# Layer 3 of a four-layer chain: split float32r product replaced by a plain float32 product on four 32-row groups of TensorE

## What is computed

```python
x = x + L0(x)   # x W^T + (x A0[label]) B0^T * 0.5      A0 rank 32, float32
x = x + L1(x)   # eight thresholds: quantise x with the step and zero point of its level
x = x + L2(x)   # x weight[adapter]^T, 1024x1024, float32
x = x + L3(x):
    B_sel = B[adapter_ids]                        # 16 x 1024
    A_sel = A[adapter_ids]                        # 1024 x 16
    Bx = einsum('bni,bri->bnr', x, B_sel)         # rank 16
    out = einsum('bnr,bor->bno', Bx, A_sel)
```

## Time and profile before

| | us |
|---|---|
| median of 3 runs (467.7 to 470.2) | 469.33 |
| the profiled execution's own time | 469.18 |
| its span, first to last instruction | 467.4 |
| PE busy | 456.0 (98%) |
| DVE busy | 414.8 (89%) |
| ACT busy | 326.7 (70%) |

### The profile page before, as it was taken

The page is one execution under the profiler, slowest core; times in us unless marked ns, Lnnn a source line. Parts: engine busy times, 40 slices in busy tenths (PEclk is TensorE's granted clock), DMA queues, the critical chain, the costliest instruction groups (busy, mean ns, idle before and its releaser), DMA issues.

```text
span 467.4 us, 7302 instructions
## 1 busy us (share of the span) xinstructions
PE 456.0 (98%) x3006; PEld 414.1 (89%) x3006; DVE 414.8 (89%) x394; ACT 326.7 (70%) x273; POOL 7.9 (2%) x17
## 2 busy tenths in 40 slices
PE   6999999999899999999999999999999999999996
PEld 5999999889898899989998899988998899988884
DVE  4789899999899997889799996899959999999983
ACT  5596999986498748957299653997249866665730
POOL 1000000000000000000000000010000000000000
PEclk9899999999999999999999999999999999999999
DMA  7983340476229534456326562193322432244242
GB/s 290 307 350 101 69 126 1 109 202 241 69 91 236 192 126 157 88 182 210 140 90 141 191 221 91 68 260 109 142 99 90 156 115 79 86 175 168 103 157 90
DMA packets 17940, 69.15 MB, mean 148 GB/s; under 512 B 2420, under 2 KB 3444, under 8 KB 13044
## 3 DMA queue, kind: packets, MB, share of 16 engines
q1 hardware_dynamic: 17044, 62.41, 37.5%
q0 software_dynamic: 864, 6.29, 7.0%
HBM read 54.01 MB, written 8.39 MB: 134 GB/s over the span
## 4 chain that ended last, share of the span: by engine, by line
PE 85%; DVE 6%; ACT 3%; issue 3%; DMA 1%; SPq 1%; DVEq 0%; ACTq 0%
PE l_ps L830 39%; PE l_ps L765 32%; PE l_ps L845 6%; DVE quant L627 2%; PE bx_ps L864 2%; DVE cand L601 2%; PE bx_ps L791 1%; DMA w_sb<-w 1%; PE l_ps L775 1%; PE l_ps L881 1%; ACT cand L438 1%; DVE quant L621 1%; ACT mask L448 1%; PE bx_ps L798 1%; PE bx_ps L871 1%
## 5 line engine op out<-in xcount | busy, mean ns | idle before, releaser
L830 PE MATMUL l_ps<-x,w_sb 128*128 128x256 f32 x896 | 197.0, 380 | 1.0 <-DVE x L678 0.6
L830 PEld LDWEIGHTS l_ps<-x,w_sb 128*128 128x128 f32 x896 | 169.2, 190 | 26.1 <-issue 3.6
L627 DVE COPY_PREDICATED quant<-mask,cand 128x2048 f32<-128x2048 int8 (+2 forms) x77 | 144.4, 1876 | 1.9 <-ACT mask L448 1.6
L438 ACT ACTIVATE cand<-x,inv_delta 128x2048 f32<-128x2048 f32 (+2 forms) x88 | 134.6, 1529 | 8.8 <-DVE quant L621 7.0
L448 ACT ACTIVATE mask<-magnitude,thr_bias 128x2048 fp8e5<-128x2048 f32 (+2 forms) x77 | 117.8, 1530 | 20.2 <-DVE quant L627 19.5
L601 DVE TENSOR_SCALAR cand<-cand,delta 128x2048 f32<-128x2048 f32 (+2 forms) x88 | 87.4, 993 | 11.8 <-ACT cand L438 11.4
L609 DVE TENSOR_SCALAR cand<-cand,lower,upper 128x2048 f32<-128x2048 f32 (+2 forms) x88 | 92.6, 1053 | 0.4
L765 PE MATMUL l_ps<-x_hi,w_hi 128*128 128x256 f32 x512 | 87.0, 292 | 4.2 <-DVE x_lo L564 1.8
L765 PE MATMUL l_ps<-x_hi,w_lo 128*128 128x256 f32 x512 | 83.0, 284 | 0.0
L765 PE MATMUL l_ps<-x_lo,w_hi 128*128 128x256 f32 x512 | 82.9, 284 | 0.0
L765 PEld LDWEIGHTS l_ps<-x_hi,w_hi 128*128 128x128 f32 x512 | 72.1, 193 | 9.3 <-issue 3.3
(11 more groups left out here) (64 smaller groups left out, 244.1 us busy)
## 6 DMA issues: line engine op xcount, KB each, us to landing
w_sb<-w SPq DMA_DIRECT2D x31, 1024.0 KB, 4.9
out<-x SPq DMA_DIRECT2D x32, 256.0 KB, 2.2
x_raw<-x SPq DMA_DIRECT2D x15, 512.0 KB, 6.3
x_lo<-x_raw POOLq DMA_DIRECT2D x6, 1024.0 KB, 8.2
a_raw<-a SPq DMA_DIRECT2D x8, 512.0 KB, 3.5
w_sb<-w SPq DMA_DIRECT2D x7, 512.0 KB, 7.4
b_sb<-b SPq DMA_DIRECT2D x8, 256.0 KB, 2.6
a_raw<-a SPq DMA_DIRECT2D x8, 128.0 KB, 6.2
```

What stands on the lines that cost most here:

```text
L438: act.activation(cand[:, c % CANDS, 0:n], x2_unit(u), ACT.Identity, bias=ROUND, scale=inv_delta[:, k:k + 1]).then_inc(rounded, 1)
L627: dve.copy_predicated(y, mask[:, m % MASKS, 0:n].bitcast(I8), t).then_inc(merged, 1)
L830: last = nc.tensor.matmul(l2_bank(b, q)[:, i * S:(i + 1) * S], w2_tile(b, o)[:, k * P:(k + 1) * P], x2[:, b % SLOTS, k * S:(k + 1) * S], s ...
```

## The change

Layer 3 becomes a plain float32 product. `a3_raw` now holds the second matrix (16 rows, padded with 16 zero rows) four times, on partitions 0-31, 32-63, 64-95 and 96-127. `bx_sum` is filled so that `sum_bx` puts Bx on all four groups of 32 as well; ACT copies it once to `bx_sb`. Quarter q of the output is then computed from partitions 32q to 32q+31 alone, so that the four quarters use four different row groups of the array; the matmuls take turns over the quarters. The splitting of `a3` and of `bx` on ACT and DVE is gone. Batch 7 takes the same way as the others: four column groups in `low_rank3`, then `drain_bx`, `sum_bx` and `copy_bx`. `b3_sb` is half as wide. `load_adapter(b)` waits for the end of layer 3 of the batch before, since layer 3 now reads `a3_raw` itself.

```diff
@@ load_adapter on SP
                 else:
                     sp.wait_ge(bx_done, b)
-                    sp.wait_ge(a3_split_done, b)
+                    sp.wait_ge(l3_done, 4 * b)
@@ ACT
-            def split_a3(b):
-                act.wait_ge(a3_loaded, (b + 1) * 16)
-                if b > 0:
-                    act.wait_ge(l3_done, 4 * b)
-                act.activation(a3_split[:, :], a3_raw[:, :], ACT.Copy).then_inc(a3_hi_done, 1)
...
-            def split_bx(b):
-                if b < B - 1:
-                    act.wait_ge(bx_sum_done, b + 1)
-                else:
-                    act.wait_ge(bx_done, b + 1)
+            def copy_bx(b):
+                act.wait_ge(bx_sum_done, b + 1)
                 if b > 0:
                     act.wait_ge(l3_done, 4 * b)
-                act.activation(bx_split[:, :], bx_whole(b), ACT.Copy).then_inc(bx_hi_done, 1)
+                act.activation(bx_sb[:, :], bx_ps[:, S:2 * S], ACT.Copy).then_inc(bx_copied, 1)
...
-            split_a3(B - 1)
-            split_bx(B - 1)
+            drain_bx(B - 1)
+            copy_bx(B - 1)
@@ DVE
-            def split_a3(b):
-                dve.wait_ge(a3_hi_done, b + 1)
-                dve.scalar_tensor_tensor(a3_split[:, :], a3_split[:, :].bitcast(F32), not_a3_hi[:, 0:1], a3_raw[:, :],
-                                         ALU.mult, ALU.add).then_inc(a3_split_done, 1)
-
-            def split_bx(b):
-                dve.wait_ge(bx_hi_done, b + 1)
-                dve.scalar_tensor_tensor(bx_split[:, :], bx_split[:, :].bitcast(F32), not_bx_hi[:, 0:1], bx_whole(b),
-                                         ALU.mult, ALU.add).then_inc(bx_split_done, 1)
@@ PE
-                n = 4 if b < B - 1 else 2
-                w = P // n
                 for k in (2 * q, 2 * q + 1):
-                    rows = slice(k % n * w, (k % n + 1) * w)
-                    last = nc.tensor.matmul(bx_ps[rows, 0:S], b3_sb[:, k, 0:w], x3[:, k * S:(k + 1) * S],
-                                            start=(k < n), stop=(k >= T - n))
+                    rows = slice(k % 4 * QUAD, (k % 4 + 1) * QUAD)
+                    last = nc.tensor.matmul(bx_ps[rows, 0:S], b3_sb[:, k, :], x3[:, k * S:(k + 1) * S],
+                                            start=(k < 4), stop=(k >= 4))
...
-            def layer3(b, q):
-                if q == 0:
-                    pe.wait_ge(bx_split_done, b + 1)
-                    pe.wait_ge(a3_split_done, b + 1)
-                on_x3 = b == B - 1 and q == 3
+            def layer3(b, order=range(4)):
+
+                pe.wait_ge(bx_copied, b + 1)
+                pe.wait_ge(a3_loaded, (b + 1) * 16)
                 for i in range(2):
-                    o = 2 * q + i
-                    last = nc.tensor.matmul(l3_bank(b, q)[:, i * S:(i + 1) * S], a3_split[:, o * P:(o + 1) * P],
-                                            bx_split[:, :], start=not on_x3, stop=not on_x3 or i == 1)
-                last.then_inc(l3_done, 1)
+                    for q in order:
+                        o = 2 * q + i
+                        rows = slice(q * QUAD, (q + 1) * QUAD)
+                        on_x3 = b == B - 1 and q == 3
+                        last = nc.tensor.matmul(l3_bank(b, q)[:, i * S:(i + 1) * S], a3_raw[rows, o * P:(o + 1) * P],
+                                                bx_sb[rows, :], start=not on_x3, stop=not on_x3 or i == 1)
+                        if i == 1:
+                            last.then_inc(l3_done, 1)
...
-            for q in LAST_ORDER:
-                layer3(B - 1, q)
+            sum_bx(B - 1)
+            layer3(B - 1, LAST_ORDER)
```

More of the change, by code:

```diff
@@ L78, in build @@
         low_parts = sb("low_parts", [P, S], F32)
-        b3_sb = sb("b3_sb", [P, T, 2 * QUAD], F32)
+        b3_sb = sb("b3_sb", [P, T, QUAD], F32)
         bx_parts = sb("bx_parts", [P, S], F32)
         a3_raw = sb("a3_raw", [P, D], F32)
-        a3_split = sb("a3_split", [P, D], F32R)
-        bx_split = sb("bx_split", [P, S], F32R)
+        bx_sb = sb("bx_sb", [P, S], F32)
         ident = sb("ident", [P, P], F32)
@@ L125, in build @@
         param_step = sem("param_step")
-        marks_ready = sem("marks_ready")
         diag_added = sem("diag_added")
@@ L151, in build @@
         x3_done = sem("x3_done")
-        a3_hi_done = sem("a3_hi_done")
-        a3_split_done = sem("a3_split_done")
         bx_done = sem("bx_done")
@@ L156, in build @@
         bx_sum_done = sem("bx_sum_done")
-        bx_hi_done = sem("bx_hi_done")
-        bx_split_done = sem("bx_split_done")
+        bx_copied = sem("bx_copied")
         l3_done = sem("l3_done")
@@ L327, in _ @@
             pool.memset(low_sum[:, :], 0.0).then_inc(sums_zeroed, 1)
-            pool.memset(bx_sum[:, :], 0.0).then_inc(sums_zeroed, 1)
-            pool.wait_ge(sums_zeroed, 2)
+            pool.wait_ge(sums_zeroed, 1)
             pool.wait_ge(fold_ready, 1)
@@ L333, in _ @@
             pool.tensor_copy(low_sum[:, 3 * QUAD:4 * QUAD], fold[:, :]).then_inc(sums_ready, 1)
-            pool.tensor_copy(bx_sum[:, 0:3 * R3].rearrange("p (q r) -> p q r", q=3),
-                             fold[:, 0:R3].unsqueeze(1).to_broadcast([P, 3, R3])).then_inc(sums_ready, 1)
+            pool.tensor_copy(bx_sum[:, :].rearrange("p (q r) -> p q r", q=4),
+                             fold[:, :].unsqueeze(1).to_broadcast([P, 4, QUAD])).then_inc(sums_ready, 1)
             def add_x(b):
@@ L473, in between @@
                         split_batch(s + 2)
[L474 to L477, removed]
+                    if j == 3 and s + 2 < B:
+                        drain_low(s + 2)
                     if j == 4 and s + 2 < B:
@@ L482, in between @@
                         drain_l0(s + 1, 0)
-                        split_bx(s - 1)
+                        copy_bx(s - 1)
                         if s + 1 < B - 1:
@@ L486, in between @@
                 elif u == LAST:
-                    if j == 2:
-                        split_a3(s - 1)
                     if j == 3:
@@ L644, in between @@
                         drain_l2(s - 1, 1)
-                    if j == 3:
-                        split_a3(s - 1)
                     if j == 4:
@@ L683, in _ @@
             dve.wait_ge(ident_ready, 1)
-            for mark, low in ((not_bx_hi, slice(QUAD, 2 * QUAD)), (not_a3_hi, slice(R3, 2 * R3))):
-                dve.tensor_reduce(mark[:, :], ident[:, :].rearrange("p (g c) -> p g c", g=2)[:, :, low],
-                                  mybir.AxisListType.XY, ALU.add, negate=True).then_inc(marks_ready, 1)
             dve.tensor_reduce(fold[:, :], ident[:, :].rearrange("p (g r) -> p r g", g=4),
@@ L725, in _ @@
             dve.wait_ge(param_step, 6)
-            dve.wait_ge(marks_ready, 2)
             for u in range(len(UNITS)):
@@ L731, in _ @@
                 finish(b - 1, q)
-            split_a3(b)
             for q in range(4):
                 drain_l2(b, q)
-            split_bx(b)
             for q in LAST_ORDER:
@@ L905, in _ @@
                     if i == 4:
-                        for q in range(4):
-                            layer3(s - 1, q)
+                        layer3(s - 1)
             for q in range(4):
@@ L915, in _ @@
             last_layer2(1, (1, 2, 3))
-            for q in range(4):
-                layer3(B - 2, q)
+            layer3(B - 2)
             last_layer2(2)
@@ L943 @@
     b3 = np.asarray(L3_cond_B).reshape(-1, R3, T, P).transpose(0, 3, 2, 1)
-    b3 = np.concatenate([b3] * 3 + [np.zeros_like(b3)], axis=3)
+    b3 = np.concatenate([b3, np.zeros_like(b3)], axis=3)
     a3 = np.asarray(L3_cond_A).transpose(0, 2, 1)
-    a3 = np.concatenate(([a3] * 3 + [np.zeros_like(a3)]) * 2, axis=1)
+    a3 = np.concatenate([a3, np.zeros_like(a3)] * 4, axis=1)
     arrays = {
@@ L957 @@
         "w2": tiles_of_weights(L2_cond_weight).reshape(-1, 4, 2, P, T * P).transpose(0, 1, 3, 2, 4),
-        "b3": b3.reshape(-1, P, T * 2 * QUAD),
+        "b3": b3.reshape(-1, P, T * QUAD),
         "a3": a3,
```

11 lines of the change are left out of this document (removed).

## The result

| | before | after |
|---|---|---|
| median, us (5 runs each) | 469.27 (467.7 to 470.2) | 472.22 (471.56 to 473.26) |
| profiled execution's own time | 469.18 | 472.22 |
| its span | 467.4 | 470.4 |

The ratio is 1.0079, with a 95% interval from 1.0056 to 1.0102: slower by more than 0.5%, as forecast, and 0.2 us from the forecast time. That nearness is luck. Two errors of opposite sign cancel in it, and the rows tell them apart.

What follows compares the result with a forecast made beforehand. PE's queue was taken to bound the kernel from 81 us on. Layer 3 in batches 0 to 6 (+2.0) and the last batch (+1.2) made +3.2 us on 469.18, so 472.4; range 469.0 to 476.0.

Steps and rivals of the forecast that it cites:

- What bounds the kernel: Whole kernel: from 81 us on PE's queue sets the time; DVE's removed splits, 14.1 us busy, are worth nothing.
- Layer 3, batches 0 to 6: Layer 3 on PE: 16 float32 passes in four row groups cost 1.24 against 0.96 us, +0.28 a batch, +2.0 for seven.
- The row of the identity passes: Four passes after `low_rank3` of batch 7, after a switch with a full load ahead: 1.06 us, taken as layer 3's price.
- the way back: Tile behind layer 3: leaving the split array costs another 0.18 us, as after `low_rank3` (3.06 instead of 2.88).
- `low_rank3` of batch 7, held by DVE's add: End of the kernel: its last quarter waits for DVE's add at 459.45, so it ends at 460.10, 0.43 earlier.
- The last batch: Batch 7: layer 3 starts 0.54 us later and quarters end together, so DVE's first add comes +1.17 us later.
- `load_adapter` at nothing: SP's queue: two load issues, 0.53 us each, ahead of the stores cost nothing; the loads have 2 us or more cover.
- The rival of the late adapter load: Batch 7: late batch 6 stores delay DVE's adds, or `b3` comes late: +1 us on the forecast, 473.4; chance 0.03.
- Serial loads: Layer 3: row groups' weight loads go one at a time, 2.30 us a batch, sum +11.1, 480.3; chance 0.10.
- no overlap: Layer 3: the four row groups do not overlap, 3.46 us a batch, sum +19.9, 489.1; chance 0.05.
- Free switch: Layer 3: row-group loads run ahead under full-width tiles, 0.86 us a batch; with the end +0.4, 469.6; chance 0.12.
- The base: Whole kernel: the forecast was added to the profiled execution's 469.18 us, leaving out the 0.15 higher median of 469.33.

Runs made afterwards that it cites:

- before_no_dve_split: Kernel before without DVE's halves of the two splits, low parts left out of layer 3: 468.53 us, ratio 1.0002 to before.
- layer3_twice: Changed kernel with layer 3's eight matmuls issued twice in batches 0 to 6: 479.05 us, ratio 1.0223 to the kernel before.
- one_row_group: Changed kernel with all eight layer 3 matmuls on partitions 0 to 31 in place of four row groups: 496.84 us, ratio 1.0606 to before.
- two buffers: Changed kernel with two buffers for the second matrix, so the adapter load is issued well ahead of the stores: 472.26 us, ratio 1.0063 to before.
- after_filled_gap: Changed kernel with eight small identity matmuls, results unused, in PE's wait at 9.6 us: 471.97 us, ratio 1.0081 to before.
- quarter_by_quarter: Changed kernel with layer 3's loops swapped, both halves of a quarter before the next quarter: 472.86 us, ratio 1.0073 to before.

## Why the prediction was right, and where it was not

- *What bounds the kernel.* Right. DVE lost 12.8 us of work for nothing, and the chain of waits is as full of PE as before. The 0.4 us wait for DVE in layer 2 stayed where the earlier trace rows put it. `before_no_dve_split` confirms it from the other side, with the same 371.52 us from the first pass of layer 2 to the end of layer 3 of batch 6.
- *Layer 3, batches 0 to 6: +0.28 a batch, +2.0.* Right: +0.31 by the chain, 1.97 and 1.95 over the whole stretch in the two pairs of profiles. The row of the identity passes (1.06) gave 1.08, the way back 0.18 gave 0.19. `layer3_twice` shows the split into 0.86 and 0.41, and `one_row_group` shows that the four groups are what saves 2.56.
- *`low_rank3` of batch 7, held by DVE's add.* Right as a mechanism, and 1.48 for 1.45 where the stores are in time. In the changed kernel itself, it was wrong.
- *The last batch, +1.17.* With two buffers, DVE's first add stands 11.74 us after the end of layer 3 of batch 6, and 10.33 before: +1.41, of which 0.19 is the way back that the forecast has under layer 3. That is +1.2. So the two terms that the forecast added up, 3.2, measure 1.97 + 1.41 = 3.4 where the stores are in time.
- *The step that failed, though the time came out: `load_adapter` at nothing.* The prediction saw that two loads would be issued in front of the stores and priced them by their issues and their own deadlines, with "2 us or more" of cover. It did not price what stands behind them: DVE's adds wait for the stores to land, and a store behind the 512 KB load landed after 5.4 and not 2.2 us. The rival of the late adapter load had the place right, down to the condition that DVE's last add must slip, and its price nearly (+1; it is +1.3 in the profile, 0.7 in the trace of `after_filled_gap`, 0.3 in that of `quarter_by_quarter`), but got 0.03 of the chance. DVE's gained split, given there as a reason against, could not help: DVE was waiting for the DMA.
- *The rivals on layer 3.* Serial loads and no overlap: out, by layer 3's 1.08 us where they had 2.30 and 3.46, and by the 18.4 us of loads in 5.6; `one_row_group` shows what no overlap would have cost. Free switch: out, by the 0.41.
- *The base.* The forecast was added to an execution with 3.4 us of half clock at its start; the median execution after had none. This took 1.6 us off and hid the failed step: +3.2 was forecast, +3.0 seen, 4.19 is the change's own. That the time came out within 0.2 us is luck; that layer 3 and the last batch came out is not.

## What to carry to other kernels

A replacement on a full TensorE queue is worth only what its own pieces in the chain of waits differ by: here eight float32r matmuls (0.96 us) against four float32 passes a group (0.86) and the switch in and out (0.41), and the 14.1 us that it freed on DVE, which was not the bound, were worth nothing. When a load's wait moves, look beyond its own deadline at what is queued behind it, and at who waits for those transfers to land; stores first, or a second buffer, gave back 0.7 us by the medians and 1.3 in the trace. If the runs of a kernel differ by the granted clock of one stretch, compare at the same clock, or fill the gap in front of it.

## What was not expected of the hardware

- The order of the matmuls over the row groups is free: with both matmuls of a group, that is four passes, next to each other in the program, four groups took 1.09 us against 1.08 in turns. Within one group the same 16 passes take 3.64 us with the entry.
- A stretch of 3.6 us in which PE was busy throughout with 32-row matmuls was followed by the lower clock (0.50) in four of seven cases, every second one; the same matmuls spread over four row groups never were, and neither were the 16 further passes of `layer3_twice`. PE's busy share does not tell of this. Why every second one is open.
- The half clock at the start came in some executions of one kernel and not in others. Of the ten profiles without the extra matmuls five show it from 11.9 to 15.1 us (0.50 to 0.58), after PE had been busy 1.48 to 1.73 us of the 3.50 from 8.0 to 11.5; the other five do not (1.00), after 1.51 to 1.85. With eight small matmuls in the gap, none of the three profiles shows it, and the times of each of the three kernels lie within 0.6 us (24 executions in all). What picks the executions stays open.
- A 256 KB store issued right behind a 512 KB load on the same queue landed after 5.4 us, and after about 2.3 with nothing in front. Whether the load's bytes or its place make the difference in full was not measured apart; with the same bytes issued after the stores, the wait fell to 0.34 us.
